# Two attentions: the maximum chunks of a step stand behind its value matmuls instead of between the pairs of scores

## What is computed

```
# layer 0 (full), q, k, v from low-rank projections
scores = einsum("bhtd,bhsd->bhts", q, k) / sqrt(8);  attn = softmax(scores);  y = einsum("bhts,bhsd->bhtd", attn, v)
# layer 1 (causal)
scores = where(causal, einsum("bhqd,bhkd->bhqk", q, k), -inf);  attn = softmax(scores / sqrt(8));  ctx = attn @ v
...
# each followed by a residual and a layer norm; between them an expert FFN,
# behind them six blocks of windowed attention and a gated FFN, and a last layer norm
```

## Time and profile before

| | |
|---|---|
| Time, median of 3 runs | 7047.55 us (7045.57 to 7049.45) |
| The profiled execution | 7049.76 us, its span 7047.9 us |
| Mean granted TensorE clock | 0.856 |
| Busy, whole span | PE 5366.3 us (76%), DVE 4602.4 (65%), ACT 3341.3 (47%), POOL 2648.0 (38%) |
| Full attention, maxima of a group to the last value matmul | about 174 to 1108 us |
| Causal attention, the same | about 1620 to 2333 us |

### The profile page before, as it was taken

How to read it: one execution, slowest core, us unless ns; L and a number is a source line. 1 busy time by engine, 2 the same in 40 slices (tenths; PEclk the granted TensorE clock), 3 DMA queues, 4 the chain that set the end, 5 groups by cost and what they waited for, 6 DMA issues and landing times. The chain is left out here.

```text
span 7047.9 us, 227710 instructions
## 1 busy us (share of the span) xinstructions
PE 5366.3 (76%) x94976; PEld 3173.1 (45%) x95234; DVE 4602.4 (65%) x9701; ACT 3341.3 (47%) x6812; POOL 2648.0 (38%) x2353
## 2 busy tenths in 40 slices
PE   5888885447777468888888888888888888888874
PEld 1222221123333145555555555555555555555552
DVE  5777773456656457666676676667667666776664
ACT  1555553213444235555555555555555555555542
POOL 0000000000000055555665655556665555665640
PEclk9999996678999678888888988888888888888885
DMA  3000000021110010001000100010001000010000
GB/s 99 15 15 14 14 10 0 27 74 29 20 19 15 16 41 24 24 27 36 19 23 24 39 24 24 24 35 22 24 24 36 27 24 24 28 29 24 24 23 15
DMA packets 88204, 185.23 MB, mean 26 GB/s; under 512 B 18278, under 2 KB 44710, under 8 KB 87462
## 3 DMA queue, kind: packets, MB, share of 16 engines
q1 hardware_dynamic: 83180, 182.88, 9.9%
q10 hardware_dynamic: 4896, 0.84, 0.1%
HBM read 54.08 MB, written 27.26 MB: 12 GB/s over the span
## 5 line engine op out<-in xcount | busy, mean ns | idle before, releaser
L369 DVE TENSOR_REDUCE a_mpart<-a_pr 128x1 f32<-128x512 f32 (+2 forms) x1904 | 1104.8, 628 | 477.7 <-PE a_pr L454 272.0
L610 ACT ACTIVATE a_probs<-a_ps 128x1024 f32<-128x1024 f32 (+3 forms) x896 | 802.2, 932 | 836.7 <-PE a_ps L472 440.1
L1322 ACT ACTIVATE w_probs<-w_pa,w_nm,w_rqs 128x64 f32<-128x64 f32 x3072 | 971.1, 415 | 126.1 <-DVE w_nm L1470 126.1
L1315 ACT ACTIVATE w_sq<-w_pr 128x512 f32<-128x512 f32 x768 | 466.3, 607 | 899.6 <-DVE w_sinb L1458 899.6
L472 PE MATMUL a_ps<-a_QS,a_KS 128*128 128x512 bf16 (+3 forms) x1719 | 502.3, 374 | 274.9 <-ACT a_probs L610 149.6
L1244 PE MATMUL w_pr<-w_xc,w_w 128*128 128x256 f32 (+1 forms) x1152 | 458.2, 578 | 292.3 <-issue 292.3
L454 PE MATMUL a_pr<-a_KS,a_QS 128*128 128x512 bf16 (+3 forms) x1815 | 606.3, 379 | 94.7 <-DMA a_QS<-a_norows 78.4
L1058 POOL TENSOR_TENSOR w_probs<-w_probs,w_rden 128x512 f32<-128x512 f32 x384 | 393.4, 1046 | 540.3 <-DVE w_rden L1480 540.3
L1032 POOL TENSOR_TENSOR w_sinb<-w_sinb,w_tabk 128x512 f32<-128x512 f32 x384 | 489.2, 1274 | 283.8 <-DVE w_sinb L1458 283.8
L1458 DVE STREAM_SHUFFLE w_sinb<-w_pr 128x512 f32<-128x512 f32 x768 | 561.7, 731 | 0.0
L336 POOL COPY a_V<-a_vals 128x288 f32 (+1 forms) x32 | 14.3, 456 | 1433.0 <-PE a_po L490 1432.8
(11 more groups left out here) (221 smaller groups left out, 9916.5 us busy)
## 6 DMA issues: line engine op xcount, KB each, us to landing
w_Vp<-w_V SPq DMA_DIRECT2D x192, 384.0 KB, 3.6
w_Vp<-w_V SPq DMA_DIRECT2D x192, 128.0 KB, 3.4
a_QS<-q_parts SPq DMA_DIRECT2D x34, 384.0 KB
a_KS<-k_parts SPq DMA_DIRECT2D x34, 384.0 KB
q_parts<-a1p_part SPq DMA_DIRECT2D x48, 128.0 KB, 1.9
k_parts<-a1p_part SPq DMA_DIRECT2D x48, 128.0 KB, 1.8
q_parts<-a2p_part SPq DMA_DIRECT2D x48, 128.0 KB, 1.8
k_parts<-a2p_part SPq DMA_DIRECT2D x48, 128.0 KB, 1.8
```

The costliest lines, as they stand in the source:

```text
L369: nc.vector.reduce_max(mpart[:, h, qt, kc:kc + 1], p_r[:, at["chunk", k] % 3, 0:width], AX_X).then_inc(max_read, 1)
L610: nc.scalar.activation(probs[:, s % 2, 2 * pair:2 * pair + 2, c0:CH], p_s[:, pair, :, c0:CH], ACT.Exp, scale=SM_SCALE).then_inc(exped, 1)
L1315: nc.scalar.square(sq[:, u, :, :], UNIT_BANK[u][:, :, :]).then_inc(S[f"sq{u}"], 1)
L1322: op = nc.scalar.activation(probs[:, g, t, c, :], s_of(g)[:, t, c, :], ACT.Exp, bias=nm[:, g, t, c:c + 1], scale=scale_of(g)[:, t, c:c + 1])
```

## The change

In the step of TensorE, the first two chunks of a step stood between the first and the second pair of scores, the third between the second pair and the value matmuls, and the rest behind these. The waits for the banks of the first three stood ahead of the scores. Now all chunks of the step stand behind the value matmuls, each behind the wait for its own bank. The other engines keep their instructions and order, and the order of the chunks among themselves, the ring of banks and share stay as they were.

```diff
@@ step(s, g, b, v, vb, loads) of TensorE @@
                     if s == NS - 1:
                         pe.wait_ge(m_stored, (g + 2) * 48)
-                    for k in todo[0:2]:
-                        bank_free(("chunk", k), v)
                     next_score(s, g, b, 0)
-                    for k in todo[0:2]:
-                        max_chunk(k, vb)
                     pe.wait_ge(exped, g * (2 * NS) + 2 * s + 2 + FIRST)
                     if s == 0:
                         pe.wait_ge(v_ready, g + (BUFS + 1) + FIRST)
                     if kt == 0:
                         pe.wait_ge(o_kept, g * 2 + hq + FIRST)
-                    for k in todo[2:3]:
-                        bank_free(("chunk", k), v)
                     next_score(s, g, b, 1)
-                    for k in todo[2:3]:
-                        max_chunk(k, vb)
                     weigh(s, b)
-                    for k in todo[3:]:
+                    for k in todo:
                         bank_free(("chunk", k), v)
                         max_chunk(k, vb)
                     if s == 1:
                         turn_out(g * 2 - 1, 0, g)
```

## The result

| | before | changed |
|---|---|---|
| Time, median (range) | 7046.56 us (7045.44 to 7049.45) | 7158.81 us (7155.04 to 7163.93) |
| Ratio, 95% interval | | 1.0159 (1.0142 to 1.0177) |
| Span of the profiled execution | 7047.9 us | 7153.2 us |
| Full attention, from the first transposition of maxima of the loop (L464) to the last | 15 groups, 58.08 us each | 63.06 us each |
| Causal attention, the same | 44.19 us each | 45.76 us each |

The change costs 112 us where 119 were forecast. The traces differ by 105.3. The last transposition of maxima of the full attention comes 78.9 us later than before, and from the first to the last of the causal attention it takes 729.2 us in place of 703.2, 26.0 more. The two make up 104.9.

A forecast was written before the change was run, and what follows sets the result against it. It took a ring of bank waits, 2.93 us a step, as the bound, with no engine full. Full attention +81 and causal +38 on 7049.76 made 7169, less 2.2 for the median: 7167 us, range 7122 to 7214.

The forecast's parts named there:

- gap: Full attention, step without chunks that contains the wait for the next group's maxima; forecast to keep its length, 6.59 us.
- S0: The score matmuls of pair 0 in a step; step lengths run from one to the next, four-chunk steps forecast 3.36 us.
- step 14: Full attention, the step behind the wait for maxima, at half clock: 4.98 us before, forecast 5.2, ends 4.7 and 5.8.
- step 4: Causal attention, six chunks and a turn_out: 5.07 us before, forecast 6.13, +1.06.
- step 11: Causal attention, one of ten steps worked out in the same way: forecast +0.18 us a group.
- c0: First chunk of a step, chunks being numbered from zero; forecast to start 1.95 us after the value matmuls' predecessor scores end.
- Rival 3: VectorE sets the pace in either order, so nothing changes: 7048 us, chance 0.03.
- Rival 4: The chunk burst runs through, the fourth chunk finding its bank free 0.65 after the first: faster, 6970 us, chance 0.03.
- the ring of the prediction: Old full-attention step: fourth chunk, its reduction, second scores, third chunk, value matmuls, fourth chunk again; 1.18 + 0.75 + 1.00 = 2.93 us.
- Rival 2: ScalarE waits cover more causal bursts, or TensorE sees freed banks sooner than 1.18: +78, 7125 us, chance 0.09.
- Rival 1: New waits delay the granted clock's return by one step in each of 32 groups: +50, 7217 us, chance 0.08.
- S1: The score matmuls of the second pair in a step; in the causal six-chunk step forecast 1.71 us after the first pair.

The follow-up runs named there:

- e6: Changed kernel with each chunk's reduction over only the first half of its columns: 6983.68 us, ratio 0.9915.
- e3: Kernel before, with only the third chunk moved behind the value matmuls and its bank wait no longer ahead of the scores: 7196.59 us, ratio 1.0221.
- e4: Kernel before, same matmul order, but each of the first three chunks waits for its bank directly ahead of itself: 6941.71 us, ratio 0.9859.
- e10: The changed kernel timed again, unaltered, against the kernel before: 7157.70 us, ratio 1.0164.
- e2: Kernel before, with the new order in the causal attention only and the old order in the full one: 7083.87 us, ratio 1.0059.

## Why the prediction was right, step by step

| Step or term | forecast | changed kernel |
|---|---|---|
| Full: four chunks | 3.36 | 3.36 |
| five chunks | 3.97 | 3.95 |
| gap, from S0 of step 13 | 6.59 | 6.60 (601.28 to 607.88) |
| step 14, half clock | 5.20 | 5.07 to 5.74, in one group 4.69 |
| group | 63.03 | 63.06 (62.9 and 63.4 in turn) |
| full attention | +81 | +78.9 |
| Causal: step 5, 6, 7, 8 | 4.29, 3.83, 3.45, 4.06 | 4.29, 3.82, 3.45, 4.07 |
| step 4 | 6.13 | 5.73 |
| step 11 | 3.00 | 1.91 with the early return of the clock, 3.11 with the late |
| group | 46.87 | 45.05 to 46.57 |
| causal attention | +38 | +26.0 |

**The mechanism.** It holds as put: VectorE frees c0's bank 1.17 to 1.18 after c0, and in a burst on three banks the fourth chunk pays what is over. e6 shows it by size: a reduction that is 0.27 shorter takes 0.27 off the step of four and twice that off the step of five, to 0.01 us of the forecast. e3 and e4 show it by place: with the same number of reductions and almost the same order, the time goes from 155 above to 100 below before with where the waits stand.

**Rival 3** (VectorE's rate) is out: VectorE rests 0.87 in a step, and e4 has shorter steps with the same reductions. **Rival 4** (the burst runs through) decides at c3 0.65 behind c0; it is 1.17. That the old order itself loses time on banks is what the ring of the prediction says; e4 shows it, at 100 us. **Rival 2** had two parts. TensorE does not see a freed bank sooner (1.17 to 1.18), and the full attention lost what was forecast. The causal part did lose less, but for the most part by the clock and not because waits for ScalarE cover the bursts. **Rival 1** (the clock) has the wrong sign for the changed kernel. The clock in the steps stayed at 1.00 and, behind the gap, it had the higher value of 0.83 or more in nine of 15 causal groups, where before it had so in two (0.69 to 0.73 in the others). In the full attention it was 0.83 and 0.69 in turn from the fourth group on, where it was 0.75 to 0.76 before, and step 14 came out on both sides of its forecast. The Trainium skill (TensorE: Matmul & The Clock Gate, "A second HAM failure mode: psum-queue depth-cycling") has the clock oscillate when each iteration cycles through banks with short idles; here TensorE waits for a bank in each step with chunks, the granted clock from 575 to 603 is 1.00, and the trace does not agree.

**What was mis-sized** is the causal term, 38 for 26. Step 11 is more than half of it, 0.6 to 0.7 of 1.1 us a group in the mean. I took its matmuls at half clock as in the trace of before. In the stretch from 2064.98 on, with the clock at 0.69, it takes 3.11; in that from 2019.59 on, with 0.83, 1.91 (2023.30 to 2025.21, one record of the first matmul missing):

```profile
2068.60 1.06 PE L472 MATMUL a_ps<-a_QS,a_KS 128*128 128x512 bf16 x2
...
2071.71 0.49 PE L472 MATMUL a_ps<-a_QS,a_KS 128*128 128x384 bf16 x2
```

Step 4 is the other part: S1 stands 1.41 after S0 where I had 1.71, and the burst and the transposes took 0.10 less; step 3 gives 0.1 of it back, since the next S0 comes later than forecast. The steps were right to 0.02 where only banks decided, and off where ScalarE or the clock did. The bounds that I kept, 1.3 to 3.5 a group, held the 1.57.

**What was luck.** By its parts, as the two traces have them, the forecast is 14 too high (105 for 119), by the medians 7 (112; 115 in e10). The difference is scatter between executions, so that the number came out closer than the parts did is luck. And the causal term has a part that the forecast had no means to know: the same causal code costs 26 in one program and 36.5 in e2.

## What to carry to other kernels

When a pool of n buffers is served in order, write the ring down: from filling a buffer to the work that stands behind the wait for it. A wait costs what of its latency is not covered by other work between the two, so put each wait directly ahead of its own user and not ahead of unrelated work; here that alone was worth 1.4%. Filling the buffers in a burst of more than n exposes what is left of the latency when the burst reaches buffer n + 1 (0.5 us for the fourth chunk here), and spacing them out helps only as long as it does not break up matmuls that run side by side.

## What the runs showed of the hardware that I had not expected

- TensorE can stand still with work at hand and nothing to wait for that the profile shows: four holes of 1.47 to 2.16 us in e2, each beginning 0.1 to 0.4 us after the granted clock had gone from 1.00 to 0.50. About 76 other falls under work had no hole, so the cause is not shown.
- The same causal code took 729 us in one program and 740 in another. The lengths of its groups repeat in a pattern (45.4, 46.5, 48.0 in e2; 46.3, 45.4, 46.5, 45.4, 45.1 in the changed kernel), which went with the clock behind the gap of each group and, for the 48.0, with the holes. Which pattern a program gets was not settled.
- Two fp32 value matmuls of 32 columns (0.99 us) cost TensorE as much as four (1.00).
